# A block's first matmuls in another order, and a table read earlier by two engines

## What is computed

```python
def _geglu(h):
    a, g = jnp.split(h, 2, axis=-1)
    return a * jax.nn.gelu(g, approximate=False)
# E = 12 experts, D = 256, HS = 512, HR = 768
ys = _geglu(xf @ Ws1 + bs1) @ Ws2 + bs2                 # the shared part, all rows
logits = (xf @ Wr + br) / TAU
top_val, top_idx = jax.lax.top_k(logits, 2)             # two experts a token
top_w = jax.nn.softmax(top_val, axis=-1)
...
h = jnp.einsum('nd,edh->enh', xf, We1) + be1[:, None, :]
yE = jnp.einsum('enh,ehd->end', _geglu(h), We2) + be2[:, None, :]
x + ys + (the two chosen experts' yE, weighted)
```

## Time and profile before

| | us |
|---|---|
| time before, median of 3 runs | 1064.05 (1063.83 to 1067.2) |
| the profiled execution, own time | 1065.91 |
| its span in the profile | 1064.3 |
| TensorE busy in the span | 948.2 (89%) |
| VectorE busy | 715.9 (67%) |
| ScalarE busy | 569.6 (54%) |

### The profile page before, as it was taken

The page is one execution under the profiler, slowest core; times in us unless marked ns, Lnnn a source line. Parts: engine busy times, 40 slices in busy tenths (PEclk is TensorE's granted clock), DMA queues, the critical chain, the costliest instruction groups (busy, mean ns, idle before and its releaser), DMA issues.

```text
span 1064.3 us, 26714 instructions
## 1 busy us (share of the span) xinstructions
PE 948.2 (89%) x7515; PEld 696.4 (65%) x7515; DVE 715.9 (67%) x1842; ACT 569.6 (54%) x1276; POOL 372.4 (35%) x537
## 2 busy tenths in 40 slices
PE   5578899999998888978899789999899999999996
PEld 4223444444453346767788678888688888888885
DVE  4776778888787654647686566776546577667753
ACT  3125555655555573323444556766546566667653
POOL 5210212254544362157000334444223444434342
PEclk9779999999999998989899989999999999999998
DMA  4552424273562131247644552545225445535232
GB/s 149 137 101 71 104 69 111 64 188 94 121 161 63 63 140 60 71 157 240 218 150 132 162 131 45 138 131 141 41 33 130 114 78 141 130 48 145 43 52 41
DMA packets 107926, 117.30 MB, mean 110 GB/s; under 512 B 20397, under 2 KB 99961, under 8 KB 107649
## 3 DMA queue, kind: packets, MB, share of 16 engines
q1 hardware_dynamic: 87168, 67.97, 24.0%
q0 software_dynamic: 20064, 47.20, 17.8%
q10 hardware_dynamic: 560, 0.53, 0.1%
HBM read 73.91 MB, written 38.87 MB: 106 GB/s over the span
## 4 chain that ended last, share of the span: by engine, by line
PE 39%; issue 5%; DMA 5%; DVE 4%; ACT 1%; DVEq 1%; SPq 1%; ACTq 1%; POOL 0%; POOLq 0%
PE ff_psH L2273 23%; PE ff_psY L2288 13%; DMA ff_xrow<-expert_in 2%; PE ff_psX L2223 2%; DVE ff_actf L2499 1%; PE ff_psH L2238 1%; DMA ff_xrow<-xn 1%; DVE ff_actl L2492 1%; DMA expert_in<-ff_zeros 1%; PE ff_psY L2253 1%; DMA out_dram<-ff_x 1%; DVE xl L2482 0%; ACT ff_gel L2353 0%; ACT xh L2339 0%; SPq L1966 0%
## 5 line engine op out<-in xcount | busy, mean ns | idle before, releaser
L2273 PE MATMUL ff_psH<-xh,ff_wx 128*128 128x256 f16 (+1 forms) x1776 | 272.0, 264 | 24.8 <-DVE ff_actf L2499 7.6
L2273 PE MATMUL ff_psH<-xl,ff_wx 128*128 128x256 f16 (+1 forms) x888 | 226.0, 264 | 0.0
L1126 DVE TENSOR_REDUCE fast_negm<-fast_psS 128x2 f32<-128x512 f32 x256 | 168.3, 686 | 70.9 <-PE fast_psS L514 69.6
L886 ACT ACTIVATE fast_PT<-fast_psT 128x512 f32<-128x512 f32 x256 | 147.2, 596 | 104.7 <-PE fast_psT L546 104.5
L2273 PEld LDWEIGHTS ff_psH<-xh,ff_wx 128*128 128x128 f16 x1776 | 168.5, 99 | 46.8 <-issue 21.6
L2208 POOL DMA_INDIRECT out_dram<-ff_ysc,ff_trow x78 | 124.8, 1600 | 204.0 <-ACT ff_ysc L2395 187.6
L2499 DVE SCALAR_TENSOR_TENSOR ff_actf<-ff_psH,ff_b1T,ff_gel 128x256 f32<-128x256 f32 (+1 forms) x234 | 105.6, 454 | 105.4 <-ACT ff_gel L2353 103.1
L2353 ACT ACTIVATE ff_gel<-ff_psH,ff_b1T 128x256 f32<-128x256 f32 (+1 forms) x234 | 104.8, 450 | 88.0 <-PE ff_psH L2273 73.3
L2288 PE MATMUL ff_psY<-ff_wx,ff_acth 128*128 128x256 f16 x792 | 132.0, 273 | 0.1
L2348 ACT ACTIVATE ff_acth<-ff_actf 128x256 f16<-128x256 f32 (+1 forms) x282 | 110.5, 392 | 37.2 <-DVE ff_actf L2499 35.4
L514 PE MATMUL fast_psS<-fast_Kz,fast_Qs 128*128 128x512 f16 x256 | 101.3, 401 | 32.3 <-DVE fast_negm L1126 23.7
(11 more groups left out here) (276 smaller groups left out, 1676.1 us busy)
## 6 DMA issues: line engine op xcount, KB each, us to landing
ff_st<-in_L_ffn_We_dram POOLq DMA_DIRECT2D x12, 1536.0 KB, 8.2
ff_xrow<-expert_in SPq DMA_DIRECT2D x41, 256.0 KB, 2.8
ff_st<-in_L_ffn_We_dram POOLq DMA_DIRECT2D x12, 768.0 KB, 9.7
fast_Qs<-qstk SPq DMA_DIRECT2D x48, 128.0 KB
fast_xbuf<-in_x_dram SPq DMA_DIRECT2D x8, 512.0 KB, 5.0
fast_words<-in_mask_BxSxS_bk_dram SPq DMA_DIRECT2D x8, 512.0 KB, 3.8
fast_xres<-in_x_dram SPq DMA_DIRECT2D x8, 512.0 KB, 4.1
out_dram<-fast_x1s SPq DMA_DIRECT2D x8, 512.0 KB, 5.1
```

The costliest lines, as they stand in the source:

```text
L886: nc.scalar.activation(PT[:, n % NPT, :], psT[n % 2][:], ACT.Exp).then_inc(sem["exp_done"], 1)
L1126: nc.vector.tensor_reduce(negm[:, two(b), t, 2 * p:2 * p + 2], src, AX.X, ALU.max, negate=True).then_inc(sem["max_done"], 1)
L2273: mm = nc.tensor.matmul(psH[j % stage.banks][:, (half + 1) * NB - rows:(half + 1) * NB], a[:, dt, lo:lo + P], x[:, dt, NB - rows:], start= ...
```

## The change

First, `ffn` on TensorE. The first half of a block's first pair is no longer six matmuls in the order high, low, high behind a wait for `xl`. It is four matmuls on `xh` behind a wait for `xh`, then a wait for `xl`, then the two matmuls on `xl`. All other matmuls keep their order. Second, ScalarE and VectorE read all twelve words in the last shared block, three after each of its four pairs, and `experts` gets them as `places`.

```diff
         def ffn(stage, m, wa, wb, more, rows=NB, between=None):
             n = stage.pairs
-            stage.until(pe, "xl", of(stage, "xl", m, 1))
+
+            def hidden(j, half, terms, begins, ends):
+                lo = (half * n + j) * P
+                for dt in range(DT):
+                    for i, (a, x) in enumerate(terms):
+                        mm = nc.tensor.matmul(psH[j % stage.banks][:, (half + 1) * NB - rows:(half + 1) * NB], a[:, dt, lo:lo + P],
+                                              x[:, dt, NB - rows:], start=(begins and dt == 0 and i == 0),
+                                              stop=(ends and dt == DT - 1 and i == len(terms) - 1))
+                return mm
+            of_high, of_low = [(wa[0], xh), (wa[1], xh)], [(wa[0], xl)]
+            stage.until(pe, "xh", of(stage, "xh", m, 1))
             for j in range(n):
-
                 stage.until(pe, "act", of(stage, "act", m, j + 1 - stage.banks))
-                for half in range(2):
-                    lo = (half * n + j) * P
-                    terms = [(wa[0], xh), (wa[0], xl), (wa[1], xh)]
...
+                if j == 0:
+                    hidden(j, 0, of_high, True, False)
+                    stage.until(pe, "xl", of(stage, "xl", m, 1))
+                    hidden(j, 0, of_low, False, True)
+                for half in range(0 if j else 1, 2):
+                    mm = hidden(j, half, [of_high[0], of_low[0], of_high[1]], True, True)
...
         shared_blocks(act, shared_block, LAST_PIECES, NSH - 1)
-        shared_block(NSH - 1, (expert, 0))
+        places = []
+
+        def next_places(j):
+            for k in range(E // SH_PAIRS):
+                next_of(act, places)
+        act.wait_ge(table_ready, 1)
+        shared_block(NSH - 1, (expert, 0), next_places)
...
-        experts(act, None, expert_rows, high_piece, unrolled=True)
+        experts(act, None, expert_rows, high_piece, unrolled=True, places=places)
...
         spare_rows()
-        shared_block(NSH - 1, (expert, 0))
+        places = []
+
+        def next_places(j):
+            for k in range(E // SH_PAIRS):
+                next_of(dve, places)
+        dve.wait_ge(table_ready, 1)
+        shared_block(NSH - 1, (expert, 0), next_places)
...
-        experts(dve, None, expert_block, low_piece, unrolled=True)
+        experts(dve, None, expert_block, low_piece, unrolled=True, places=places)
```

More of the change, by code:

```diff
@@ L1978, in place_of, with next_of @@
         return rest & (PLACE - 1), rest >> PLACE.bit_length() - 1, (value & (OVER - 1)) >> 1
+    def next_of(eng, places):
+        if len(places) < E:
+            places.append(place_value(eng, len(places)))
     def experts(eng, before, body, piece=None, halves=True, unrolled=False, places=None, over=None):
@@ L2263, in ffn @@
             n = stage.pairs
-            stage.until(pe, "xl", of(stage, "xl", m, 1))
+            def hidden(j, half, terms, begins, ends):
[8 more added lines that the diff above has]
+            stage.until(pe, "xh", of(stage, "xh", m, 1))
             for j in range(n):
                 stage.until(pe, "act", of(stage, "act", m, j + 1 - stage.banks))
-                for half in range(2):
-                    lo = (half * n + j) * P
-                    terms = [(wa[0], xh), (wa[0], xl), (wa[1], xh)]
-                    for dt in range(DT):
-                        for i, (a, x) in enumerate(terms):
-                            mm = nc.tensor.matmul(psH[j % stage.banks][:, (half + 1) * NB - rows:(half + 1) * NB], a[:, dt, lo:lo + P],
-                                                  x[:, dt, NB - rows:], start=(dt == 0 and i == 0), stop=(dt == DT - 1 and i == 2))
+                if j == 0:
[4 more added lines that the diff above has]
+                    mm = hidden(j, half, [of_high[0], of_low[0], of_high[1]], True, True)
                 mm.then_inc(stage.sem["h_mm"], 1)
@@ L2320, in next_place @@
         def next_place():
-            if len(places) < E:
-                places.append(place_value(pe, len(places)))
+            next_of(pe, places)
         pe.wait_ge(table_ready, 1)
@@ L2363, in ffn, with shared_block @@
                 beside(n - 1)
-        def shared_block(m, more=None):
-            ffn(shared, m, bs1T[:, SH_PAIRS:], more or (shared, m + 1))
+        def shared_block(m, more=None, beside=None):
+            ffn(shared, m, bs1T[:, SH_PAIRS:], more or (shared, m + 1), beside)
         def high_piece(e, use, u, done, k, begins):
@@ L2523, in low_piece, with shared_block @@
             nc.vector.tensor_tensor(wx[u][1][:, cols], st[u][:, cols], wx[u][0][:, cols], ALU.subtract).then_inc(w_low, 1)
-        def shared_block(m, more=None):
-            ffn(shared, m, bs1T, more or (shared, m + 1), add_shared)
+        def shared_block(m, more=None, beside=None):
+            ffn(shared, m, bs1T, more or (shared, m + 1), add_shared, beside)
         shared_blocks(dve, shared_block, 0, 2)
```

## The result

The changed kernel takes **1057.29 us** in the median of 6 runs (1054.43 to 1061.85). The kernel before takes 1064.35 in the median of its 6 (1062.97 to 1067.2). The ratio is 0.9931, 95% interval 0.9908 to 0.9953, that is 5.0 to 9.8 us. The forecast was 1058.3 with a range from 1056.5 to 1062.5. The profiled execution of the changed kernel took 1056.36 us, its span is 1054.7.

The account below looks back on a forecast made before the run. TensorE, busy 948.2 us or 89% of the span, was taken to bound the kernel. Terms of 3.5 + 1.7 + 0.3 + 0.3 = 5.8 us off the 1064.05 median gave 1058.3 us, range 1056.5 to 1062.5.

Parts of the forecast that it names:

- The order of the products: At full blocks behind half blocks, four products on `xh` start before `xl` is ready: 8 x 0.44 = 3.5 us gained.
- the 8 places: Block starts where a half block is followed by a full one and TensorE waited for `xl`, 3.7 us in all.
- the stall of 0.16: Wait of TensorE forecast to remain before the first product on `xl` in a full block, after the 0.44 us gain.
- Does the block keep the gain?: Claim that full blocks keep their 0.44 us, since VectorE is needed only 3.9 us later and no `ff_actf` wait is listed.
- The loads at six starts: Starts of experts 2, 4, 6, 7, 9 and 11: removing ScalarE's load shifts everything by 0.28 us each, 1.7 us in all.
- expert 5: At expert 5's start VectorE's own load is the one that counts; removing it gains 0.3 us.
- the loads' time stays: Rival, 18%: at experts' starts the load only covered late instructions, so only the product order gains 3.5 us, giving 1060.5.
- Expert 0: At expert 0's start VectorE's 0.28 us idle behind a load goes, and TensorE takes all of it: 0.3 us.
- The loads in the last shared block: Twelve added loads each on ScalarE and VectorE run beside other work there and cost 0, bounds 0 to 4.9 us.
- The slower case: Rival, 4%: moved ScalarE and VectorE code causes new TensorE issue stalls, 5.7 us each with slow clock; two give 1069.7.

Follow-up runs that it names:

- the first four kernels of the experiments: Against the kernel before: block number masked with 127 only, 1101.05 us; with that mask, whole change 1094.83, product order alone 1100.64, early loads alone 1097.21.
- the one with the mask: The kernel before plus one register operation that masks the block number with 127, nothing else changed; 1101.05 us, ratio 1.002.

## Why the prediction was right, step by step

**The order of the products, 3.5 us.** In the profile after, the distance from the last product of the half block to the first of the full one fell at the 8 places from 5.9 us in sum to 2.1: 3.8 instead of 3.5, with the stall of 0.16 ahead of the first product instead of behind the fourth. What the prediction left out stands at "Does the block keep the gain?": I asked only for waits for VectorE later in the block, and found none listed. The rows' transposes stand in it too, and rows come at a time that TensorE doesn't set. In the experiments this alone gave back 1.9 of 2.4 us. That the term held is luck: it rests on a coupling I hadn't seen, by which the other part of the change brings the rows' issue forward. On one point I was warned by a row and didn't use it: the earlier trace rows shows TensorE waiting for such a DMA, at expert 0.

**The loads at six starts, 6 x 0.28 = 1.7, and expert 5, 0.3.** Right in mechanism and a little small. Expert 2 gave 0.30, expert 5 0.33, and the sum of these waits from expert 1 on fell from 6.64 to 4.39: 2.25 instead of 2.0. Without the loads 2.2 us went, with the loads doubled 2.4 came. The rival "the loads' time stays" (18%) falls with that. The Trainium skill's floor of about 600 ns for a `tensor_load` (DMA: Bandwidth & Descriptors, "Latency and other measured facts") is no floor here: the medians in the changed kernel are 279 and 308 ns, and 0.31 us a place was gained. By that figure seven places would have gained 4.2 us, an estimate. Loads of 0.66 to 0.97 us do occur, in the kernel with twelve in a row.

**Expert 0, 0.3 us.** Wrong. The step that failed is "then idles 0.28 us with nothing to wait for, behind a load; that idle goes". The load ran within the adds: it ended at 590.12 (589.8 + 0.33), the adds at 590.43, and the idle came behind these. That is what I used in the next paragraph to price the loads at nothing; it can't have been both beside the adds and on the path behind them. The idle stayed at 0.30. And "TensorE waits 1.81 us there, so it takes all of it" left out that the adds wait for `ff_x`, so that what TensorE gains before them is lost there. The products' gain at expert 0's full block did come, 0.37 us, and the wait for expert 1's weights behind it didn't take it back (start to start 6.58 and 6.46 us). But the wait for `ff_actf`, 0.7 us longer, ate both: 27.90 us from expert 0 to expert 1 became 27.99.

**The loads in the last shared block, 0.** Right: 120.10 us of shared blocks beside 121.20, and 12 loads in one row change nothing measurable, although ScalarE's took twice what I had priced.

**The slower case.** No new stall of some microseconds came. The one of the earlier trace rows is there as before, 4.02 us at 766.35.

**The total.** 1057.29 lies 1.0 under the forecast, and the interval of the gain, 5.0 to 9.8 us, holds 5.8. The stretches give 5.9, but 1.1 of it lie in the shared blocks, where I had forecast nothing and nothing is shown. From expert 1 on it is 4.9: 3.5 from the starts of 7 full blocks, 2.25 from the loads, less 0.45 of longer waits for rows and 0.4 that I can't place. From expert 0 to 1 it is -0.1, where I had forecast 0.7. So the mechanisms gave 4.8 of the 5.8. The rest of the measured 7.1 us lies where the change has no mechanism, and in the later sessions the whole change was worth 3.5 to 4.2 us against the kernel before, with intervals that both hold 5.8. The sum came out closer than its steps deserve, by luck: two sizes were a little small, one term was not there, and one cost was missing.

## What to carry to other kernels

Where a wait on another engine is taken away, follow the block to its next operand from memory: a transfer issued at a fixed point, used just in time, takes the gain back, and its issue must be moved along with its use. A scalar load at the top of a branch cost its whole time here on the engine that the others wait for, and nothing in the stretch before, where engines wait anyway. Two parts of a change should be tried apart and together, since here they gave 0.2 and 2.5 us alone and 4.05 as one, expert 1's half block left out. And a stretch of TensorE is compared together with its granted clock: behind a long wait the same products took up to 2.4 us more in one profile than in another.

## What the runs showed of the hardware

**A small transfer beside a large one.** Rows of 256 KB, issued by SyncE, landed 2.5 to 3.5 us after their issue where nothing large was under way, and up to 9.85 us after it beside the 2.25 MB of weights. Their landing went from 3.0 to 8.9 us as the issue moved from 0.28 to 0.42 us behind that of the weights. TensorE's waits for them ended 9.6 to 10.1 us after their issue in the first four kernels of the experiments.

**TensorE's clock behind a wait.** Behind 6.5 us of wait for weights the half-width products started 0.11 instead of 0.055 us apart for 26 to 55 products, with a granted clock of 0.80 and 0.64 over 8 us in the two windows above; behind 3.0 us of wait for rows it was 0.50 over the next 5 us, behind 1.9 us of the same wait 1.00.

**TensorE slow beside GpSimd's scatters.** In all kernels of the three later sessions the shared blocks took 141 to 144 us instead of 121, and the stretch before them 8 to 14 more. The same 26 us of GpSimd's scatters, in the kernel before and in the one with the mask (columns as above):

```profile
474.00:500.00 26.00, 22.18 (x198) 19.12 (x197) 19.08 (x61) 8.99 (x23) 19.91 (x21) 0.93 0.67 238
```

```profile
486.00:512.00 26.00, 11.99 (x82) 8.18 (x80) 4.09 (x9) 2.50 (x7) 19.91 (x21) 0.69 0.39 136
```

GpSimd does the same 19.91 us of work, but TensorE gets 82 matmuls instead of 198 and the DMA moves 136 GB/s instead of 238. The gaps on TensorE are put down to "issue", 0.7 to 2.8 us each, for example

```profile
497.02 0.37 PE L2273 MATMUL ff_psH<-xh,s1h 128*128 128x256 f16 x1 [1.19 <-issue]
```

so it waits for nothing that the profile shows; that its instructions come late is a reading and not shown. The granted clock of the stretch is 0.69 instead of 0.93. The kernel before was as slow in these sessions, so the mask isn't the cause. What it is stays open; no experiment was made on it. At 34 us (1098.5 to 1099.4 against 1064.35) it costs almost five times what the change brings.
